# Moving number tables into an earlier stage, 16-bit one-hots, and a bias folded into a matmul as an extra row

## Chip, cores and metric

The kernel runs on one core of one Trainium2 chip. The metric is device time in microseconds (us), from one launch to its end; lower is better. Before the change it took 3679.51 us, the median of three runs.

## What is computed

Four layers follow one another on 3125 nodes with 256 features each; every layer works on the layernorm of x and adds its result to x.

```python
x = x + _L0_gnn_ref(_layernorm(x), edge_index, ...)   # two graph attention layers: 8 heads, then 1 head
x = x + _L0_ffn_ref(_layernorm(x)[None], ...)[0]      # 8 experts, top 2, 256 -> 512 -> 256, exact gelu
x = x + _L1_gnn_ref(_layernorm(x), src, dst, ...)     # attention over 100000 edges, then an MLP
x = x + _L1_ffn_ref(_layernorm(x)[None], ...)[0]      # shared MLP plus 4 experts, top 2
```

The part of the last layer that the change touches, and the routing of the second:

```python
# L1_ffn: E = 4 experts, 256 -> 128 -> 64 -> 256
o = jnp.einsum('ebag,ego->ebao', h, eW3) + eb3[:, None, None, :]
...
gates = softmax(x @ gW + gb); topv, topi = top_k(gates, 2); topw = softmax(topv)
gated = sum(sel * topw)          # out = shared + gated

# L0_ffn: E = 8 experts
top_vals, top_idx = jax.lax.top_k(logits, 2)
w = jax.nn.softmax(top_vals, axis=-1)
```

## The kernel before

The nodes are padded to 3200, that is 25 tiles of 128 (`NT`), or 5 chunks of 5 tiles (`NTC`, `TC`). x stays on chip (`X`), as does a transposed copy of the layer's input (`XT`). Each stage is a block with one instruction stream per engine, written out by hand; semaphores order them, and a stage ends with a barrier of all engines, after which POOL clears the stage's semaphores. The chain of a stage on VectorE (DVE) goes through `link`, which makes the next instruction wait for the one before.

The stages in order are: the edge lists are sorted and counted into a dense matrix of edge counts; graph layer with eight heads; graph layer with one head (`stage_gat_one_head`, L1053); first experts (`stage_experts`, L1395); attention (`stage_attention`, L1903); tail (`stage_tail`, L2211).

**One-head layer.** TensorE (PE) adds up weighted messages, chunk after chunk, 25 weight tiles each (L1319); DVE makes the weights (L1177) into a ring of six. At its start POOL makes a padding column (L1266, L1268) and then the greatest of all partitions (`partition_all_reduce`, L1271). After that POOL has nothing more to do in the stage. The router's logits, top values and indices of each chunk are made beside the next chunk.

**First experts.** The nodes are sorted by expert on the chip. POOL first makes number tables with `iota` (L1530 to L1537): numbers 0 to 127, three tables of node places, a table of spare rows; then a triangular table (`before`, L1540) from a table of ones that DVE sets (L1753). DVE waits for five of these before it reads the expert numbers (L1756); PE waits for all six before it ranks (L1567, L1569). DVE then works out each node's row, cuts it into a tile number and a place in the tile (L1787), and makes one-hots by comparing the number table with them:

```python
for j in range(2):
    hi    = (num[:, 0:TILES] == cutf[:, 1, half])     # L1790, 128x1425, bf16 out
    named = hi * parts[...]                            # L1793, twice, 128x1425
    lo    = (num[:, :] == cutf[:, 0, half])            # L1796, 128x3200
```

Here `num`, `cutf` and `parts` are 32-bit floats; the second operand is one number repeated over 57 or 128 elements. PE multiplies these one-hots (L1578), which gives the node of each row; DVE ends the list (L1808 to L1813), and POOL gathers the rows by indirect DMA (L1545). PE waits for all expert weights (`s_wt`) before the first tile's first layer (L1594). The weights, 8 MB, and two bias tables repeated over all partitions, 2 MB and 1 MB (L1500, L1501), are loaded by SP from the stage's start; then comes the diagonal of the counts (L1502), on which DVE waits at L1818. 57 tiles of rows pass through both layers, one after another.

**Tail.** For every chunk c the PE stream holds: the up matmuls of the MLP (L2357), the down matmuls (L2404), and, of chunk c-1, the last layer: `moe_up` (L2379) and `moe_down` (L2418) of the shared net "s" and of experts 0 to 3, interleaved. After the last chunk's MLP (c = 4) come chunk 3's experts, with the flips and router logits (L2336) of chunk 4 between them, and then chunk 4's experts. PSUM has a ring of three banks for up and three for down: PE can run three tiles ahead of the engine that reads. ScalarE (ACT) reads the up results (L2423, L2436); DVE reads the down results (L2498, L2556, L2559). DVE's order within a chunk c:

```python
norm(2, c - 1); finish_projection(c + 2); route(c - 1); norm(1, c + 2); add_features(c); finish_mlp(c)
add_expert_biases(c - 1)          # L2542: 20 instructions, L2546: the shared bias
if c == LAST_C: norm(2, LAST_C)
finish_moe(c - 1)                 # after the loop: route(LAST_C), add_expert_biases, finish_moe
```

`route` makes logits to weights of experts and needs two exponentials of ACT (L2445, L2449). ACT takes chunk 4's root (L2441) before chunk 3's expert reads, and chunk 4's exponentials among chunk 4's expert reads. The expert biases of the third layer (`tw.e3_b`) lie in all 128 partitions, loaded as a 512 KB broadcast during attention (L2173).

## Time and profile before

| | us |
|---|---|
| three runs | 3667.97, 3679.51, 3680.68 |
| median | 3679.51 |
| profiled execution, its own time | 3674.5 |
| its span, first to last instruction | 3672.7 |
| PE busy | 3043.4 (83% of the span) |
| DVE busy | 2850.6 (78%) |
| ACT busy | 2209.2 (60%) |
| POOL busy | 350.1 (10%) |

Of the span, the one-head layer takes 1481 to 1819, the first experts 1819 to 2186, attention 2186 to 3234 and the tail 3234 to 3673. All times of the trace count from the first instruction. A busy share says little by itself: each stage has its own limit, so the views below are of stretches. In a timeline a row stands for one instruction or a merged run of them, with its start, its duration, engine, line and tile names; the bracket tells how long the engine had been idle before it and whose end released it. PE's granted clock is given as a share of its full speed, 1.00 for 2.4 GHz and 0.50 for 1.2 GHz.

### The profile page before, as it was taken

The numbers are of one execution on the slowest core, as the hardware profiler recorded it, in microseconds if no ns is written. First come the engines' busy times: TensorE is split into PE (matmuls) and PEld (weight loads), VectorE is DVE, ScalarE is ACT, GpSimd is POOL, SyncE is SP. The second block draws the span as 40 slices with busy tenths as digits, with TensorE's granted clock in tenths as the row PEclk, the third lists the DMA queues.
The fourth block names the chain that finished last, engine by engine and source line by source line (L and its number), as shares of the span: only waits on it lengthen the run. The fifth ranks groups of instructions, "written<-read, shape, count | busy, mean of one in ns | idle before, by whom it ended". The sixth has DMA issues, their size and how long they took to land. (4 is left out here: it accounts for less than half of the span.)

```text
span 3672.7 us, 45213 instructions
## 1 busy us (share of the span) xinstructions
PE 3043.4 (83%) x15824; PEld 1562.9 (43%) x15826; DVE 2850.6 (78%) x3424; ACT 2209.2 (60%) x3171; POOL 350.1 (10%) x490
## 2 busy tenths in 40 slices
PE   3216766888888888899669969999999999969987
PEld 2212333333333333688547643333333333357765
DVE  8887987799999998455454459999999999934554
ACT  3101467899999998111123348889888888824332
POOL 0000000001111112000034400010111111000000
PEclk8557998999999999999879989999999999989998
DMA  2000234444443443444232154333333333210000
GB/s 55 0 0 23 78 145 156 125 117 117 113 117 108 117 113 90 177 144 151 76 114 65 57 194 112 88 88 89 90 89 88 89 89 89 69 62 22 8 8 14
DMA packets 191828, 325.64 MB, mean 89 GB/s; under 512 B 33388, under 2 KB 137046, under 8 KB 191632
## 3 DMA queue, kind: packets, MB, share of 16 engines
q1 hardware_dynamic: 175408, 294.36, 26.7%
q0 software_dynamic: 16224, 28.69, 2.8%
q8 instruction: 120, 1.97, 0.2%
q14 instruction: 76, 0.62, 0.1%
HBM read 254.53 MB, written 61.88 MB: 86 GB/s over the span
## 5 line engine op out<-in xcount | busy, mean ns | idle before, releaser
L921 PE MATMUL acc<-weights_then_messages,messages 128*64 128x400 f32 x3200 | 608.3, 513 | 93.7 <-DVE weights_then_messages L995 66.3
L2006 PE MATMUL acc<-weights,keys_and_values 128*64 128x400 f32 x3200 | 631.9, 516 | 2.4 <-DVE weights L2138 1.2
L2135 DVE SCALAR_TENSOR_TENSOR weights<-x,counts 128x1600 f32<-128x1600 f32 x304 | 555.0, 1826 | 18.0 <-ACT x L2102 7.6
L995 DVE SCALAR_TENSOR_TENSOR weights_then_messages<-rho,kappa,counts 128x800 f32<-128x800 f32 x400 | 415.0, 1082 | 4.8 <-PE acc L921 4.4
L2099 ACT ACTIVATE x<-scores 128x800 f32<-128x800 f32 x496 | 408.7, 851 | 13.5 <-PE scores L1993 13.4
L921 PEld LDWEIGHTS acc<-weights_then_messages,messages 128*64 128x64 f32 x3200 | 206.9, 137 | 491.7 <-issue 210.1
L1993 PE MATMUL scores<-q,keys_and_values 32*128 32x400 f32 x3200 | 386.5, 552 | 32.6 <-ACT x L2097 31.8
L943 ACT ACTIVATE weights_then_messages<-rho,wx 128x800 f32<-128x800 f32 x400 | 361.9, 953 | 26.0 <-DVE weights_then_messages L1000 17.2
L1000 DVE TENSOR_TENSOR weights_then_messages<-weights_then_messages,counts 128x1600 f32<-128x1600 f32 x200 | 365.0, 1825 | 5.4 <-ACT weights_then_messages L948 5.4
L2006 PEld LDWEIGHTS acc<-weights,keys_and_values 128*64 128x64 f32 x3200 | 195.1, 136 | 389.5 <-issue 347.9
L948 ACT ACTIVATE weights_then_messages<-weights_then_messages,kappa 128x800 f32<-128x800 f32 x400 | 360.5, 950 | 0.0
L2097 ACT ACTIVATE x<-scores,plus_minus_clip 128x800 f32<-128x800 f32 x304 | 283.4, 932 | 80.4 <-PE scores L1993 78.1
L651 PE MATMUL acc<-weights_then_messages 128*128 128x400 bf16 x1024 | 240.0, 370 | 102.4 <-ACT acc L627 59.1
L2102 ACT ACTIVATE x<-x,plus_minus_clip 128x800 f32<-128x800 f32 x304 | 296.9, 977 | 0.0
L1319 PE MATMUL acc<-weights_then_messages,weights 128*128 128x257 f32 x1250 | 278.7, 383 | 16.6 <-DVE weights L1177 12.7
L2126 DVE TENSOR_SCALAR x<-x 128x800 f32<-128x800 f32 (+1 forms) x400 | 267.4, 669 | 24.7 <-ACT x L2099 24.3
L1319 PEld LDWEIGHTS acc<-weights_then_messages,weights 128*128 128x128 f32 x1250 | 237.6, 191 | 52.4 <-DVE weights L1177 13.2
L1993 PEld LDWEIGHTS scores<-q,keys_and_values 32*128 32x128 f32 x3200 | 126.4, 185 | 288.5 <-ACT x L2097 213.7
L669 DVE TENSOR_TENSOR weights_then_messages<-dst_number_twofold,dst_of 128x6400 bf16<-128x6400 f16 x64 | 223.1, 3486 | 0.0
L625 ACT COPY counts_out<-acc 128x400 f32<-128x400 f32 x200 | 97.8, 489 | 197.4 <-PE acc L651 155.2
L651 PEld LDWEIGHTS acc<-weights_then_messages 128*128 128x128 bf16 x1024 | 119.5, 117 | 223.0 <-issue 183.8
L1177 DVE SCALAR_TENSOR_TENSOR weights<-rho,kappa,counts 128x640 f32<-128x640 f32 x125 | 109.4, 884 | 125.9 <-PE acc L1319 125.8
(371 smaller groups left out, 3642.6 us busy)
## 6 DMA issues: line engine op xcount, KB each, us to landing
counts<-edge_counts SPq DMA_DIRECT2D x200, 400.0 KB, 3.2
counts<-edge_counts SPq DMA_DIRECT2D x400, 200.0 KB, 2.4
edge_counts<-counts_out SPq DMA_DIRECT2D x40, 1000.0 KB, 4.1
counts<-edge_counts SPq DMA_DIRECT2D x24, 1600.0 KB, 7.1
w_first<-in_L_ffn_W_dram SPq DMA_DIRECT2D x8, 512.0 KB, 9.4
w_second<-in_L_ffn_W_dram SPq DMA_DIRECT2D x8, 512.0 KB, 8.8
y<-sums POOLq DMA_DIRECT2D x32, 100.0 KB, 2.7
denominators<-sums_of_weights POOLq DMA_DIRECT2D x32, 100.0 KB, 4.0
```

Source lines behind the costliest of these rows:

```text
L651: nc.tensor.matmul(acc[:, bass.ds(bank, 1), 0:CH], hot_s[:, u % 2, g, :, s], hot_d[:, u % 2, m // TWO, :, m % TWO], start=False, stop=Fals ...
L921: ins = nc.tensor.matmul(acc[64 * o:64 * o + 64, p, h, 0:CH], msg[:, t, r % 2 * Q + q, :], w[:, T % WR, q, half(h)], start=(t == 0), stop= ...
L943: nc.scalar.activation(mx[:, T % WR, e, :], rho[:, r % 2, 2 + e, :], ACT.Relu, bias=nkap[:, t, j:j + 1]).then_inc(s_relu, 1)
L948: nc.scalar.activation(mx[:, T % WR, e, :], mx[:, T % WR, e, :], ACT.Identity, bias=kap[:, t, j:j + 1]).then_inc(s_mx, 1)
L995: nc.vector.scalar_tensor_tensor(out=w[:, T % WR, q, :], in0=rho[:, r % 2, q, :], scalar=kap[:, t, j:j + 1], in1=cbuf[:, T % CR, :], op0=A ...
L1000: nc.vector.tensor_tensor(w[:, T % WR, 2:4, :], mx[:, T % WR, :, :], cbuf[:, T % CR:T % CR + 1, :].to_broadcast([P, 2, CW]), ALU.mult).the ...
L1319: ins = nc.tensor.matmul(acc[:, d, 0:F + 1], w[:, (i * NT + t) % WR, d * P:(d + 1) * P], msg[:, t, :], start=(t == 0), stop=(t == NT - 1))
L1993: ins = nc.tensor.matmul(sc[:, (n + j // 2) % SR, j % 2, 0:CH], kT[part, r % KF, t * P:(t + 1) * P], q[part, r % 2, :], start=True, stop=True)
L2006: ins = nc.tensor.matmul(acc[64 * e:64 * e + 64, p, 0:CH], msg[:, t, r % KF * 2 + p, D * e:D * e + 2 * D], w[:, U % WR, 2 * p + e, :], sta ...
L2099: nc.scalar.activation(out, pair, ACT.Exp, scale=D ** -0.5).then_inc(s_read, 1)
L2102: nc.scalar.activation(ex[:, U % XR, 0:2, :], ex[:, U % XR, 0:2, :], ACT.Exp, bias=ten[:, 1:2]).then_inc(s_ex, 1)
L2135: ins = nc.vector.scalar_tensor_tensor(out=w[:, U % WR, :, :], in0=out, scalar=EXP_HI, in1=counts, op0=ALU.min, op1=ALU.mult)
```

## The change

It does four things. (1) The number tables, the ones and the triangular table move from the experts' start into the one-head stage: POOL's five iotas and the triangular table stand behind `partition_all_reduce`, and DVE makes the ones and 16-bit copies of two tables at the end of chunk 1's weights. (2) The experts' waits for the tables go, and the one-hots read 16-bit tables and 16-bit row parts. (3) The third bias of the tail's experts becomes row 64 of the weight tile, against a row of ones under the hidden layer; the 20 DVE instructions per chunk go, and the shared bias is added earlier, behind `norm(2, c)`. (4) Chunk 4's routing moves: on DVE between chunk 3's experts 0 and 1, on ACT ahead of chunk 3's last up read.

```diff
@@ -1047,6 +1047,12 @@
...
+        self.num = core.sb(ctx, "numbers", [P, P])
+        self.num16 = core.sb(ctx, "numbers_16", [P, P], BF16)
+        self.parts16 = core.sb(ctx, "place_of_node", [P, 3, NT], BF16)
+        self.spare = core.sb(ctx, "spare_row", [P, TILES])
+        self.before = core.sb(ctx, "lower_ones", [P, P], BF16)
+        self.every = core.sb(ctx, "ones_16", [P, P], BF16)
...
@@ -1083,6 +1089,8 @@
...
+        parts = core.sb(ctx, "parts", [P, 3, NT])
+        s_const, s_const16 = core.sem("numbers_made"), core.sem("numbers_16_made")
...
@@ -1269,6 +1277,18 @@
...
+                nc.gpsimd.iota(route.num[:, :], pattern=[[1, P]], base=0, channel_multiplier=0,
+                               allow_small_or_imprecise_dtypes=True).then_inc(s_const, 1)
+                for j in range(2):
+                    nc.gpsimd.iota(parts[:, j, :], pattern=[[1, NT]], base=TILES + j * NT, channel_multiplier=0,
+                                   allow_small_or_imprecise_dtypes=True).then_inc(s_const, 1)
+                nc.gpsimd.iota(parts[:, 2, :], pattern=[[0, NT]], base=0, channel_multiplier=1,
+                               allow_small_or_imprecise_dtypes=True).then_inc(s_const, 1)
+                nc.gpsimd.iota(route.spare[:, :], pattern=[[P, TILES]], base=0, channel_multiplier=1,
+                               allow_small_or_imprecise_dtypes=True).then_inc(s_const, 1)
+                pool.wait_ge(s_const16, 1)
+                nc.gpsimd.affine_select(out=route.before[:, :], in_=route.every[:, :], compare_op=ALU.is_ge, fill=0.0, base=-1,
+                                        pattern=[[1, P]], channel_multiplier=-1).then_inc(s_const, 1)
...
@@ -1365,6 +1385,11 @@
...
+                        if i == 1 and t == NT - 1:
+                            dve.wait_ge(s_const, 5)
+                            nc.vector.memset(route.every[:, :], 1.0).then_inc(s_const16, 1)
+                            nc.vector.tensor_copy(route.num16[:, :], route.num[:, :]).then_inc(s_const16, 1)
+                            nc.vector.tensor_copy(route.parts16[:, :, :], parts[:, :, :]).then_inc(s_const16, 1)
...
@@ -1435,11 +1460,7 @@
...
-        before = core.sb(ctx, "lower_ones", [P, P], BF16)
-        every = core.sb(ctx, "ones_16", [P, P], BF16)
-        num = core.sb(ctx, "numbers", [P, P])
-        parts = core.sb(ctx, "place_of_node", [P, 3, NT])
-        spare = core.sb(ctx, "spare_row", [P, TILES])
+        before, every, num, num16, parts, spare = route.before, route.every, route.num, route.num16, route.parts16, route.spare
...
@@ -1450,7 +1471,7 @@
...
-        cutf = core.sb(ctx, "row_parts", [P, 2, S2])
+        cutf = core.sb(ctx, "row_parts", [P, 2, S2], BF16)
...
@@ -1462,9 +1483,9 @@
...
-        (s_wt, s_num, s_set, s_dve, s_pair, s_e, s_both, s_rank, s_tile, s_lo, s_named, s_ix, s_node,
+        (s_wt, s_dve, s_pair, s_e, s_both, s_rank, s_tile, s_lo, s_named, s_ix, s_node,
...
-             "weights_in", "numbers_made", "constants_set", "dve", "pair_ready",
+             "weights_in", "dve", "pair_ready",
...
@@ -1527,18 +1548,6 @@
...
-                nc.gpsimd.iota(num[:, :], pattern=[[1, P]], base=0, channel_multiplier=0,
-                               allow_small_or_imprecise_dtypes=True).then_inc(s_num, 1)
-                for j in range(2):
-                    nc.gpsimd.iota(parts[:, j, :], pattern=[[1, NT]], base=TILES + j * NT, channel_multiplier=0,
-                                   allow_small_or_imprecise_dtypes=True).then_inc(s_num, 1)
-                nc.gpsimd.iota(parts[:, 2, :], pattern=[[0, NT]], base=0, channel_multiplier=1,
-                               allow_small_or_imprecise_dtypes=True).then_inc(s_num, 1)
-                nc.gpsimd.iota(spare[:, :], pattern=[[P, TILES]], base=0, channel_multiplier=1,
-                               allow_small_or_imprecise_dtypes=True).then_inc(s_num, 1)
-                pool.wait_ge(s_set, 2)
-                nc.gpsimd.affine_select(out=before[:, :], in_=every[:, :], compare_op=ALU.is_ge, fill=0.0, base=-1,
-                                        pattern=[[1, P]], channel_multiplier=-1).then_inc(s_num, 1)
...
@@ -1562,7 +1571,6 @@
...
-                pe.wait_ge(s_num, 6)
...
@@ -1749,9 +1757,7 @@
...
-                nc.vector.memset(both[:, NT, :], 0.0)
-                nc.vector.memset(every[:, :], 1.0).then_inc(s_set, 2)
-                dve.wait_ge(s_num, 5)
+                link(nc.vector.memset(both[:, NT, :], 0.0))
...
@@ -1787,13 +1793,13 @@
...
-                    link(nc.vector.tensor_tensor(hi[:, half, :], num[:, 0:TILES].unsqueeze(1).to_broadcast([P, NT, TILES]),
+                    link(nc.vector.tensor_tensor(hi[:, half, :], num16[:, 0:TILES].unsqueeze(1).to_broadcast([P, NT, TILES]),
...
-                    nc.vector.tensor_tensor(lo[:, half, :], num[:, :].unsqueeze(1).to_broadcast([P, NT, P]),
+                    nc.vector.tensor_tensor(lo[:, half, :], num16[:, :].unsqueeze(1).to_broadcast([P, NT, P]),
...
@@ -2164,7 +2170,7 @@
...
-        self.e3, self.e3_b = core.sb(ctx, "w_expert_3", [P // 2, NE, F]), core.sb(ctx, "b_expert_3", [P, NE, F])
+        self.e3 = core.sb(ctx, "w_and_b_expert_3", [P // 2 + 1, NE, F])
...
@@ -2199,10 +2205,10 @@
...
-                bring(self.e3[:, e, :], a["L1_ffn_eW3"][e])
+                bring(self.e3[0:P // 2, e, :], a["L1_ffn_eW3"][e])
...
-            bring(self.e3_b[:, :, :], a["L1_ffn_eb3"].partition_broadcast(P))
+            bring(self.e3[P // 2:P // 2 + 1, :, :], a["L1_ffn_eb3"].unsqueeze(0))
...
@@ -2261,7 +2267,7 @@
...
-        eh2 = arena[0:P // 2, at_eh2:at_eh2 + NE * TN].rearrange("p (e n) -> p e n", n=TN)
+        eh2 = arena[0:P // 2 + 1, at_eh2:at_eh2 + NE * TN].rearrange("p (e n) -> p e n", n=TN)
...
@@ -2280,11 +2286,12 @@
...
-        (s_up, s_act, s_down, s_read, s_flip, s_turn, s_lg, s_logit, s_tb, s_feat, s_b2, s_eb, s_sb, s_dve, s_e1, s_e2, s_iota,
+        (s_up, s_act, s_down, s_read, s_flip, s_turn, s_lg, s_logit, s_tb, s_feat, s_b2, s_sb, s_dve, s_e1, s_e2, s_iota,
...
-             "bias_p_added", "features_added", "bias_2_added", "expert_biases_added", "shared_bias_added", "dve", "exp_1", "exp_2",
+             "bias_p_added", "features_added", "bias_2_added", "shared_bias_added", "dve", "exp_1", "exp_2",
...
+        s_row = core.sem("row_of_ones")
...
@@ -2430,7 +2437,7 @@
...
-                        to, b = (eh1[:, net, half(h)], tw.e1_b[:, net:net + 1]) if l == 1 else (eh2[:, net, half(h)],
+                        to, b = (eh1[:, net, half(h)], tw.e1_b[:, net:net + 1]) if l == 1 else (eh2[0:P // 2, net, half(h)],
...
@@ -2532,23 +2539,17 @@
             link(ins)
             link(nc.vector.tensor_tensor(wf[:, c % 2, :, :], hot[:, 0, :, :], hot[:, 1, :, :], ALU.add))
 
-        def add_expert_biases(dve, c):
-
-            for e in range(NE):
-                for j in range(TC):
-                    node = X[:, c * TC + j, :]
-                    if e:
-                        dve.wait_ge(s_eb, (c * NE + e - 1) * TC + j + 1)
-                    nc.vector.scalar_tensor_tensor(out=node, in0=tw.e3_b[:, e, :], scalar=wf[:, c % 2, j, e:e + 1], in1=node,
-                                                   op0=ALU.mult, op1=ALU.add).then_inc(s_eb, 1)
-            dve.wait_ge(s_eb, (c + 1) * NE * TC)
+        def add_shared_bias(dve, c):
+
+            dve.wait_ge(s_norm[1], (c + 1) * TC)
             nodes = X[:, chunk(c), :]
             nc.vector.tensor_tensor(nodes, nodes, tw.s3_b[:, :].unsqueeze(1).to_broadcast([P, TC, F]), ALU.add).then_inc(s_sb, 1)
 
-        def finish_moe(dve, c):
-
-            dve.wait_ge(s_sb, c + 1)
-            for net in ["s"] + list(range(NE)):
+        def finish_moe(dve, c, nets):
+
+            if "s" in nets:
+                dve.wait_ge(s_sb, c + 1)
+            for net in nets:
                 for j in range(TC):
                     n, node = down_no[(net, c, j)], X[:, c * TC + j, :]
                     dve.wait_ge(s_down, n + 1)
@@ -2587,6 +2588,7 @@
             @block.tensor
             def _(pe):
                 pe.wait_ge(tw.sem, tw.count)
+                pe.wait_ge(s_row, 1)
                 project(pe, 0)
                 project(pe, 1)
                 for g in range(3):
@@ -2660,18 +2662,18 @@
...
-                for n, (net, l) in enumerate(MOE_UPS):
+                            if n == len(MOE_UPS) - 2 and c == LAST_C:
+                                exp_gates(act, LAST_C)
+                                exp_pair(act, LAST_C)
+                for net, l in MOE_UPS:
...
-                    if n == 2:
-                        exp_gates(act, LAST_C)
-                    if n == 4:
-                        exp_pair(act, LAST_C)
...
+                nc.vector.memset(eh2[P // 2:P // 2 + 1, :, :], 1.0).then_inc(s_row, 1)
...
@@ -2679,6 +2681,7 @@
...
+                        add_shared_bias(dve, c - 1)
...
@@ -2687,15 +2690,15 @@
...
-                    if c:
-                        add_expert_biases(dve, c - 1)
...
-                    if c:
-                        finish_moe(dve, c - 1)
-                route(dve, link, LAST_C)
-                add_expert_biases(dve, LAST_C)
-                finish_moe(dve, LAST_C)
+                        add_shared_bias(dve, LAST_C)
+                        finish_moe(dve, LAST_C - 1, ["s", 0])
+                        route(dve, link, LAST_C)
+                        finish_moe(dve, LAST_C - 1, range(1, NE))
+                    elif c:
+                        finish_moe(dve, c - 1, ["s"] + list(range(NE)))
+                finish_moe(dve, LAST_C, ["s"] + list(range(NE)))
...
```

## Rows read from the trace of the kernel before

**Rows 1.** Page, parts 1 and 5 (busy, mean ns | idle before).
```profile
PE 3043.4 (83%) x15824; PEld 1562.9 (43%) x15826; DVE 2850.6 (78%) x3424; ACT 2209.2 (60%) x3171; POOL 350.1 (10%) x490
...
L1177 DVE SCALAR_TENSOR_TENSOR weights<-rho,kappa,counts 128x640 f32<-128x640 f32 x125 | 109.4, 884 | 125.9 <-PE acc L1319 125.8
```

**Rows 2.** Timeline, DVE, entry of the first experts.
```profile
1831.93 0.20 DVE L1756 CAST ids_f<-logits_values_ids 128x50 f32<-128x50 uint32 x1 [12.32 <-POOL spare_row L1537]
...
1860.10 0.21 DVE L1813 TENSOR_TENSOR place_of_row<-node_part,spare_row 128x57 uint32<-128x57 f32 x1
```

**Rows 3.** Timeline, POOL, and of DVE the instruction at 278.85.
```profile
1491.99 0.38 POOL L1271 PARTITION_ALL_REDUCE greatest<-top  x1 [10.20 <-issue]
...
1831.19 0.24 POOL L1530 IOTA numbers<- 128x128 f32 x1 [338.83 <-issue]
...
278.85 0.17 DVE L512 MEMSET ones<- 128x128 bf16 x1 [0.59 <-DVE keys L186]
...
286.05 0.98 POOL L485 IOTA step_number<- 128x1024 f32 x1 [179.51 <-issue]
...
317.13 0.46 POOL L592 IOTA column_number<- 128x400 f32 x1 [29.99 <-POOLq L482]
```

**Rows 4.** Timeline, PE and ACT, tail end, ahead of which PE idles.
```profile
3580.96 0.21 ACT L2441 ACTIVATE std<-std 128x5 f32<-128x5 f32 x1 [25.73 <-DVE std L2473]
...
3581.64 2.50 PE L2379 MATMUL up<-xt,w_shared 128*128 128x320 f32 x4 [9.57 <-ACT shared_hidden L2436]
...
3645.14 2.07 PE L2418 MATMUL down<-w_shared,shared_hidden 128*128 128x256 f32 x4 [10.96 <-DVE x L2556]
```

**Rows 5.** Timeline, entry of the experts; DMA issues (KB each, us to landing).
```profile
1838.55 2.95 SPq L1501 DMA_DIRECT2D keys_and_values<-in_L_ffn_b_dram  x1
...
1870.18 3.78 PE L1594 MATMUL up<-w_first,xt 128*128 x4
...
keys_and_values<-in_L_ffn_b_dram SPq DMA_DIRECT2D x1, 1024.0 KB, 14.0
```

**Rows 6.** Groups by form, DVE: count | busy us, mean ns | idle.
```profile
L669 DVE TENSOR_TENSOR weights_then_messages<-dst_number_twofold,dst_of 128x6400 bf16<-128x6400 f16 x64 | 223.1, 3486 | 0.0
L1796 DVE TENSOR_TENSOR xt<-numbers,row_parts 128x3200 bf16<-128x3200 f32 x2 | 7.0, 3486 | 0.0
L1793 DVE TENSOR_TENSOR xt<-keys_and_values,place_of_node 128x1425 bf16<-128x1425 bf16 x4 | 6.4, 1642 | 0.1
```

**Rows 7.** Timeline, DVE, biases of chunk 3 in chunk 4.
```profile
3569.21 8.00 DVE L2542 SCALAR_TENSOR_TENSOR x<-b_expert,expert_weights,x 128x256 f32<-128x256 f32 x20
3577.25 1.49 DVE L2546 TENSOR_TENSOR x<-x,b_shared 128x1280 f32<-128x1280 f32 x1
```

**Rows 8.** Windows: length, busy by engine, granted clock, DMA share, GB/s.
```profile
3582.00:3588.00 6.00, 6.00 (x13) 3.76 (x13) 1.13 (x4) 1.47 (x4) 0.00 (x0) 0.53 0.00 0
...
3645.00:3650.00 5.00, 4.86 (x12) 3.43 (x12) 1.59 (x5) 0.53 (x1) 0.00 (x0) 0.59 0.00 0
...
1880.00:2110.00 230.00, 228.13 (x998) 160.03 (x995) 100.69 (x168) 78.17 (x163) 104.16 (x107) 1.00 0.20 62
```

**Rows 9.** Timeline, PE, tail's start; group of a DVE memset.
```profile
3234.32 5.39 PE L2393 MATMUL down<-w_p,xt 128*128 128x256 f32 x12 [20.46 <-PEq L2056]
...
3241.35 4.58 PE L2393 MATMUL down<-w_p,xt 128*128 128x256 f32 x20 [1.65 <-DVE keys_and_values L2460]
...
L656 DVE MEMSET zero<- 128x400 f32 x1 | 0.4, 392 | 0.6 <-PEq L482 0.6
```

**Rows 10.** Timeline, ACT and DVE, routing of chunk 4.
```profile
3629.89 1.28 ACT L2445 ACT_TABLE_LOAD   x1
...
3631.31 1.93 ACT L2436 ACTIVATE keys_and_values<-up,b_expert 128x320 f32<-128x320 f32 x4
...
3631.44 0.17 DVE L2510 TENSOR_REDUCE per_node<-logits 128x5 f32<-128x20 f32 x1 [9.91 <-ACT logits L2445]
...
3634.88 0.18 DVE L2533 TENSOR_TENSOR expert_weights<-hot 128x20 f32<-128x20 f32 x1
```

## The prediction

> **What bounds the kernel now.** The page first: PE is busy for 83% of the span [rows 1]. Where PE is fed, taking work off another engine gives nothing; only the stretches count in which PE stands still. The change touches three: the entry of the first experts, the end of the tail and the tail's start.
>
> At the experts' entry the timeline of DVE shows one long chain. DVE stands still for 12.32 us ahead of its first cast, until POOL's spare-row table is there, and the node list ends at 1860.3 [rows 2]. POOL's timeline tells why: its first iota starts at 1831.19, and takes 0.24 us. The same kind of hole stands ahead of the iota at 286.05, in a stage that DVE had entered by 278.85, and 10.20 us stand ahead of the all-reduce at 1491.99, which comes behind other POOL operations. The iota at 317.13, with no all-reduce since the one before it, waited for the barrier alone [rows 3]. So I read that each switch between the all-reduce and the other operations costs POOL 7 to 12 us. At 1819 everybody waits for it.
>
> At the tail's end PE stands still twice: 9.57 us ahead of 3581.64, since ACT is held up in chunk 4's root (it waited 25.73 us for DVE, which was at the bias instructions), and 10.96 us ahead of 3645.14, since DVE was late with the routing and then the biases [rows 4]. In the chunks before, the bias instructions lie under PE's work.
>
> **Part 1, the tables.** POOL's tables take about 1 us, behind a switch that now falls at some 1492 to 1504, where POOL has nothing else to do. DVE adds three instructions of 0.2 us at the end of chunk 1 (about 1615), long after the tables it waits for; behind them are queued only the next weights. In this stage DVE waits longer for PE (125.9 us) than it works on weights (109.4) [rows 1], and the ring holds six, so they are covered; uncovered they would cost 0.6. POOL's iotas could hold up DVE at the layer's ramp by their own 1 us at most. I take 0, range 0 to 1.6. In the experts DVE then casts right at the start: 12.3 us earlier. PE's ranking and ACT's exponential stand behind DVE in this chain and move with it.
>
> What is late next? PE's first expert matmul at 1870.18 comes 9.9 us behind the end of the list: gather, flip, turn. With the list ready at 1848.0 it would come at 1857.9. It also waits for the weights: the last bias table was issued at 1838.55 and landed 14.0 us later, at 1852.6 [rows 5]. So the weights are no bound, by 5 us; but the first gather starts 4.6 us before they are in, and shares the DMA engines with them. That costs 0 to 4.6 us; most of the gather's time lies behind, so I take 1. SP's and POOL's later transfers of the stage keep their order. **Gain at the entry: 12.3 - 1 = 11.3 us.**
>
> **Part 2, 16-bit one-hots.** The chain has two compares of 3486 ns and six operations on 1425 elements (the four products at 1642 ns, two compares of that size taken alike): 16.8 us, nearly all on the path. They take one element per step: 3486 ns for 3200. The one row with 16-bit operands throughout does 6400 in the same time, but its number tables are kept twofold, so that both operands lie in neighbouring elements [rows 6]. Here the second operand stays one number repeated. The bounds are 0 and, with the per-element part halved, some 7.8 us. The instructions themselves are the nearest rows, as they have the repeated operand, and the fast row's extra tables would be pointless if a repeated operand were as good. I take 0. The 16-bit row parts (L1787) cost as before.
>
> The Trainium skill, "Vector Engine (DVE) Microarchitecture Reference", section 5.1, speaks against this part: it asks for a step of one in every operand and reports that one element read 16 times, in a two-source operation on 2-byte data, ran at the slow rate. By that the term is 0 too; no row here shows this case.
>
> **Part 3, the bias as a row.** The 512 KB less to load lie in attention, where SP loads ahead of use: 0. The 65th row adds no column to a matmul: 0. The shared bias, 1.49 us, stands earlier, where DVE next waits for PE's projections; covered by PE's up matmuls, 1.49 us a chunk if they were not. In chunks 1 to 3 the 8.0 us of biases were under PE's work: 0.
>
> Chunk 4 counts. The root's input comes 8.00 + 1.49 us earlier [rows 7], so ACT is free at about 3571.8, just when PE has filled its three banks (3581.64 - 9.57 = 3572.1). Of the idle 0.3 remain: **gain 9.3**. The idle also cost clock: in the 6 us after it PE was busy throughout at a mean grant of 0.53, so 2.8 us of work were lost, 3.0 with the piece before [rows 8]. **Gain 3.0.**
>
> At the tail's start there is a loss. PE now waits for the row of ones: DVE sets 2560 elements, in one partition. 400 took 392 ns, so about 2.5 us; PE starts up to 2.7 us later than at 3234.32. But it waited 1.65 us for DVE at 3241.35 anyway [rows 9]. Bounds 0 and 2.7; I take the difference of 1.1, and 0.4 since the clock rises later: **loss 1.5**.
>
> **Part 4, the router.** In the last chunk DVE has neither routing nor biases left, so PE's 10.96 us go: **gain 11.0**. Behind that idle the grant was 0.59 over 4.86 busy us: **gain 2.0** [rows 8]. But the routing now stands in chunk 4, ahead of expert 1's down reads. PE cannot pass three unread tiles. From the up matmul of expert 2's second layer on come ACT's read (about 0.5, 1.93 for four), a table load of 1.28, the exponential 0.2, the routing from L2510 to the end of L2533, 3.6, and the first tile's read, 0.4: 6.0 us [rows 10]. PE fills three tiles meanwhile, about 1.5 us (two took 2.07 at the low level [rows 4]). **New stall 4.5**; queued behind it are expert 1's last two tiles and the rest of PE's stream, and behind ACT's exponentials its last up read. Whether so short an idle costs clock no row tells: bounds 0 and 3.0, and I take a **loss of 2.0**, the smaller of the two drops seen.
>
> Tail: 9.3 + 3.0 + 11.0 + 2.0 - 4.5 - 2.0 - 1.5 = 17.3 us. Both: 28.6 us. From the profiled execution's own 3674.5 (its span of 3672.7 and 1.8 around it) that gives **3645.9 us**. The median of the three runs stands 5.0 us above that execution; seen from it, the same gain gives 3650.9, which the range must hold.
>
> **Rivals.** *A, the one-hots do run at double rate* (10%). The list is ready 7.8 us earlier still, but PE waits for the weights until 1852.6 [rows 5], and the gathers start in the thick of the loads. At most 5.3 us more than 1857.9; with the same gather delay, 4: 3642. The fast 16-bit row speaks for it, its layout against it.
>
> *B, the tail gives most of it back* (14%). DVE reaches the routing late, the stall is twice as long (9.0), costs the full 3.0 of clock and 3 us more for a second drop, the start costs 2.7: 9.3 + 3.0 + 13.0 - 9.0 - 6.0 - 2.7 = 7.6. With 11.3 that is 18.9: 3655.6; with 4.6 lost in the gathers, 3659.2. For it speaks that PE, DVE and ACT now wait for each other in turn; against it that the routing's input is ready while PE still has two up matmul groups ahead.
>
> *C, slower* (4%): the clock in the expert loop. PE is busy there for 228 of 230 us at a mean grant of 1.00 [rows 8], some 4.1 us for each of 57 tiles. At half level a tile would take up to 4 us more. If the level, after an entry under the loads, did not hold, the gain would be used up from 8 tiles on, and from 12 tiles it would be slower by 0.5%. 20 tiles give 3646 + 80 = 3726. Against it: the loop held the level throughout, and the change leaves it as it is.
>
> *D, the hole is no switch* (3%) but something that POOL does when it first works in this stage, also now, ahead of the gather. From 1848 on it would cost up to 12 us again: 3657. Against it the iota at 317.13.
>
> **How the numbers follow.** The forecast's own case has 69%. With no gather delay, no clock lost behind the new stall and a free start of the tail it gives 3641.4; with 4.6, 3.0, 2.7 and 1.6 for the one-head layer 3653.3. The median may stand 5.0 us above such a sum, as it does now, and the three runs spread over 12.7: so 3637 to 3658. For 8 in 10 I take 3636 to 3660; that holds A, nearly all of the own case and part of B. A measurement of this kernel can tell about 0.5%, 18.4 us of the median, from no change, so the border is at 3661. Faster: own case, A, and those parts of B and D that stay below it, 0.83; within: the rest of these, 0.13; slower: C, 0.04.
>
> **What would show it.** Right: DVE's first cast within 1 us of the stage's start; the first L1594 some 11 us closer to that start; L1790, L1793 and L1796 at 1642 and 3486 ns; L2542 gone; under 1 us of idle among chunk 3's shared up matmuls; one stall of about 5 us at L2418 in chunk 4 and none in the last chunk. Wrong: a hole ahead of the first gather, one-hots in half their time, a stall above 8 us, or half-level clock in the expert loop.

## The result, and the profile after

The changed kernel takes 3639.2 us (median of 4 runs, 3637.5 to 3645.2) beside 3678.9 for the kernel before on the same chip; the ratio is 0.9903, 95% interval 0.9886 to 0.9921. In a later set of five rounds it was 3641.6 beside 3679.4, ratio 0.9895 (0.9880 to 0.9910). The forecast was 3645.9, range 3636 to 3660. The profiled execution of the changed kernel took 3645.2 us (span 3643.4), the slowest of its four; the profiled one before took 3674.5. So the two traces are 29.3 us apart where the sum said 28.6; the table shows that so close a match is luck.

A first table says where this went. A stage begins with SP's first DMA issue in it; the last column runs from TensorE's first up product of chunk 3's mixture (its shared net and four experts), which stands in chunk 4, to the end of the span. All in us, one profiled execution each; "after, again" is a second run of the changed kernel, and the rows below it are the other experiments.

| kernel | one-head | experts | attention | tail | its last part |
|---|---|---|---|---|---|
| before | 338.2 | 366.4 | 1048.6 | 438.4 | 104.0 |
| after | 337.4 | 353.8 | 1049.9 | 416.6 | 82.4 |
| after, again | 337.4 | 353.6 | 1048.3 | 418.0 | 82.4 |
| b_dummy_iota | 336.5 | 351.4 | 1048.5 | 441.8 | 104.3 |
| a_twofold | 338.1 | 354.7 | 1046.6 | 416.6 | 82.3 |
| a_route_late | 336.6 | 356.6 | 1048.2 | 409.4 | 76.3 |
| a_route_late_early_exp | 336.6 | 353.6 | 1048.1 | 410.2 | 74.6 |
| a_exps_earlier | 338.3 | 354.8 | 1046.6 | 409.2 | 75.1 |
| a_64rows | 338.4 | 354.5 | 1046.5 | 428.6 | 91.5 |
| a_late_row_wait | 337.1 | 353.7 | 1046.5 | 424.7 | 89.6 |
| a_warm_front | 337.0 | 353.9 | 1046.7 | 416.3 | 82.3 |
| a_warm_reduce | 329.8 | 354.5 | 1050.2 | 416.4 | 82.4 |
| a_all_four | 328.3 | 352.5 | 1048.3 | 411.5 | 76.3 |

Between before and after: experts 12.7 us shorter, tail 21.9 shorter, attention 1.3 longer (it spreads over 4 us in kernels that do not touch it), one-head 0.8 shorter, and 4.7 us more in the stages ahead, which the change leaves alone (in the kernels that leave them alone the one-head stage starts anywhere from 1475.3 to 1485.8). So the three stages that the change touches got 35.3 us shorter, 6.7 more than the sum, and 6.0 us of drift elsewhere hid it. On the page TensorE's work has not moved, and VectorE lost 36 us of work (compare [rows 1]).

Page of the changed kernel, parts 1 and 5 (busy, mean ns | idle before).
```profile
PE 3040.4 (83%) x15825; PEld 1560.8 (43%) x15826; DVE 2815.1 (77%) x3327; ACT 2209.9 (61%) x3171; POOL 347.1 (10%) x490
...
L1185 DVE SCALAR_TENSOR_TENSOR weights<-rho,kappa,counts 128x640 f32<-128x640 f32 x125 | 109.3, 883 | 124.4 <-PE acc L1339 124.4
```
The weights of the one-head layer cost what they did: the tables added there are covered.

The experts' entry, timelines of POOL (one-head stage), then VectorE and TensorE (experts' stage, which starts at 1823.18).
```profile
1496.96 0.38 POOL L1279 PARTITION_ALL_REDUCE greatest<-top  x1 [10.46 <-issue]
1508.34 0.24 POOL L1280 IOTA numbers<- 128x128 f32 x1 [11.01 <-issue]
...
1823.38 0.20 DVE L1762 CAST ids_f<-logits_values_ids 128x50 f32<-128x50 uint32 x1
...
1831.20 1.65 DVE L1796 TENSOR_TENSOR keys_and_values<-numbers,row_parts 128x1425 bf16<-128x1425 bf16 x1
1836.00 3.48 DVE L1802 TENSOR_TENSOR xt<-numbers,row_parts 128x3200 bf16<-128x3200 bf16 x1
...
1860.26 3.46 PE L1602 MATMUL up<-w_first,xt 128*128 x4
```
The hole of 11.01 us now stands behind the all-reduce, where nobody waits. The first cast comes 0.2 us into the stage (12.65 before, [rows 2]), the one-hots take what they took [rows 6], and the first expert matmul comes 37.1 us into the stage instead of 50.9 [rows 5]: 13.8 us earlier. The last first-layer matmul comes 14.1 us earlier; 1.4 of that go back at the stage's end, which leaves 12.7. 0.6 of the 1.4 lie in the first key projections, which take 4.4 us instead of 3.8; why was not tried.

The tail's end, timelines of ACT, PE and DVE.
```profile
3563.86 0.21 ACT L2448 ACTIVATE std<-std 128x5 f32<-128x5 f32 x1 [16.30 <-DVE std L2480]
...
3589.38 1.28 ACT L2452 ACT_TABLE_LOAD   x1
3590.68 0.22 ACT L2452 ACTIVATE logits<-logits 128x20 f32<-128x20 f32 x1
...
3590.93 0.18 DVE L2517 TENSOR_REDUCE per_node<-logits 128x5 f32<-128x20 f32 x1 [4.96 <-ACT logits L2452]
...
3595.13 2.08 PE L2425 MATMUL down<-w_and_b_expert,keys_and_values 65*128 65x256 f32 x4 [4.83 <-DVE x L2560]
...
3616.58 2.42 PE L2425 MATMUL down<-w_shared,shared_hidden 128*128 128x256 f32 x10
```
Both idle times of [rows 4] are gone; one of 4.83 us is new, in chunk 4. Behind it the granted clock is low. Windows of PE: length, busy, granted clock, DMA share, GB/s.
```profile
3593.00:3595.00 2.00, 0.00 (x0) 0.71 0.00 0
3595.00:3597.00 2.00, 1.87 (x4) 0.50 0.00 0
3597.00:3599.00 2.00, 2.00 (x5) 0.50 0.00 0
3599.00:3601.00 2.00, 2.00 (x5) 0.59 0.00 0
3601.00:3603.00 2.00, 2.00 (x11) 1.00 0.00 0
```
PE was busy 5.87 us in the last three low windows at 0.50, 0.50 and 0.59: 2.8 us of work lost. The tail's start, DVE and PE, the stage starting at 3226.85:
```profile
3227.83 2.19 DVE L2676 MEMSET keys_and_values<- 1x2560 f32 x1 [7.61 <-POOL iota L2567]
...
3230.17 9.74 PE L2400 MATMUL down<-w_p,xt 128*128 128x256 f32 x32 [23.95 <-DVE keys_and_values L2676]
```
PE starts 3.3 us into the tail instead of 0.04 [rows 9], but its first up product of chunk 0 comes only 0.9 later (25.03 for 24.11). In the other kernels with this tail start it comes at 24.8 to 25.1, in one, a_route_late, at 23.9.

### The profile page after: what moved, and what is told of

Its sections match the earlier page's. It is cut to its first block and busy times, and to the rows that moved or that the text cites. A ratio compares the mean times of both kernels' runs of the same rounds, so it can differ in the third digit from the quotient of the medians.

```text
span 3643.4 us, 45117 instructions
## 1 busy us (share of the span) xinstructions
PE 3040.4 (83%) x15825; PEld 1560.8 (43%) x15826; DVE 2815.1 (77%) x3327; ACT 2209.9 (61%) x3171; POOL 347.1 (10%) x490
## 5 line engine op out<-in xcount | busy, mean ns | idle before, releaser
L1185 DVE SCALAR_TENSOR_TENSOR weights<-rho,kappa,counts 128x640 f32<-128x640 f32 x125 | 109.3, 883 | 124.4 <-PE acc L1339 124.4
```

## The experiments

Theory S: POOL pays 10 to 12 us for a switch between the all-reduce and its other operations, and part 1 gained because the switch now falls where POOL is idle. Theory R: a repeated 16-bit operand keeps VectorE at one element a step. Theory N: part 4 loses time once parts 1 to 3 are in. The rivals stand with each run. Four, four and three kernels shared a chip; times are ratios to the kernel before on that chip.

**b_dummy_iota.** On the kernel before:
```
 nc.gpsimd.partition_all_reduce(most[:, :], top_es[:, :], P, RMAX).then_inc(s_all, 1)
+nc.gpsimd.iota(small[:, :], pattern=[[0, 1]], ...)      # one column, read by nobody
```


> The kernel before with one thing added: a one-column iota on POOL right behind the one-head stage's all-reduce; every table stays in the experts' stage. Theory S (a switch): POOL pays some 10 to 12 us whenever its next work is an iota, memset or select and the one before was the all-reduce, and pays it ahead of that work wherever it stands. Then the one-column iota starts 10 to 11.5 us behind the all-reduce, POOL's first iota in the experts' stage starts within 1.5 us of the stage's first DMA issue where it was 12, the first cast is 10.5 to 11.5 us earlier in the stage, the experts' stage takes 354 to 356 us instead of 366.4, and the whole is 10 to 12.5 us shorter (about 3667). Rival D of the prediction (the hole belongs to POOL's first work of a stage, whatever was before): the first iota still stands 12 us into the stage and the whole is within 2 us of the kernel before.

3659.5 us, ratio 0.9954 (0.9938 to 0.9971), so 17 us faster, 11 to 23. POOL's timeline, both stages:
```profile
1493.02 0.38 POOL L1273 PARTITION_ALL_REDUCE greatest<-top  x1 [10.01 <-issue]
1504.26 0.14 POOL L1274 IOTA small<- 128x1 f32 x1 [10.87 <-issue]
...
1819.15 0.24 POOL L1534 IOTA numbers<- 128x128 f32 x1 [314.76 <-POOLq L1265]
```
One iota that computes nothing of use moves the hole: the tables' iota starts 0.3 us into the experts' stage (11.9 before) and the first expert matmul comes at 36.6 us, even a little ahead of the changed kernel's 37.1. Rival D is out. All that parts 1 and 2 gain at the entry is this switch, and one line gets it. The size was above the expectation: the gather came 11.7 us earlier, the matmul 14.3. From the gather's issue to the first flip it is 5.4 us instead of 7.5: gathers issued while the weights were still landing were not slower here. The total is 17 us by the medians, but 12.1 from trace to trace, and the tail, which the edit leaves alone, is 3.4 longer in this trace.

**a_twofold.** On the changed kernel, shortened (the same for the compares of 58 and for `named`, whose places are doubled too):
```
-cutf = core.sb(ctx, "row_parts", [P, 2, S2], BF16)
+cutf = core.sb(ctx, "row_parts", [P, 2, S2, 2], BF16)      # each value twice, side by side
-num16[:, :].unsqueeze(1).to_broadcast([P, NT, P]), cutf[:, 0, half].unsqueeze(2).to_broadcast([P, NT, P])
+counted(P), twice(cutf[:, 0, half, :], P)      # both seen as [P, NT, P // 2, 2]
```


> The changed kernel with the one-hots' repeated operand laid out in pairs: every row part and every place stands twice side by side, so that the innermost step of both operands is one 16-bit element and the repeat moves one dimension out; 57 columns become 58. Theory R (the prediction's ground for part 2: a 16-bit operand that is repeated with step 0 keeps the engine at one element a cycle, a pair layout does not): the 3200-element one-hot takes 1.75 to 1.9 us instead of 3.49 and the 1450-element ones 0.8 to 1.0 instead of 1.64, the first gather is issued 7 to 8.5 us earlier in the stage. Rival F (16-bit operands give this operation nothing in any layout): 3.49 and 1.67 stay. In the time even theory R gives little, 0 to 2 us, since VectorE's wait for the diagonal ends at 38 us of the stage whatever comes before it, and the first hidden layer's bias stands behind it.

3642.4, ratio 0.9912 (0.9887 to 0.9937): the same as the changed kernel. Timelines, DVE and PE:
```profile
1831.05 1.82 DVE L1814 TENSOR_TENSOR xt<-numbers,row_parts 128x3200 bf16<-128x3200 bf16 x1
1832.79 0.91 DVE L1809 TENSOR_TENSOR keys_and_values<-numbers,row_parts 128x1450 bf16<-128x1450 bf16 x1
...
1841.06 0.21 DVE L1831 TENSOR_TENSOR place_of_row<-node_part,spare_row 128x57 uint32<-128x57 f32 x1
...
1858.47 3.44 PE L1604 MATMUL up<-w_first,xt 128*128 x4 [8.79 <-DMA keys_and_values<-in_L_ffn_b_dram]
```
Theory R holds: 1.82 us for 3.48, 0.91 for 1.65. The Trainium skill, "Vector Engine (DVE) Microarchitecture Reference", section 5.1, asks for an innermost step of one in every operand, and reports the slow rate for one element read 16 times in a two-source operation on 2-byte data. The pair layout meets the first, the changed kernel's is the second, and the rows agree with both. But the list, 7.4 us earlier, buys nothing: PE waits 8.79 us for the last bias table, and starts 38.3 us into the stage. So the weights and biases are the entry's next bound, and the changed kernel stands close to it: the table landed at 35.7 us of its stage, 1.4 ahead of the first product, and in three of the runs (a_twofold, a_route_late, a_exps_earlier) it landed at 37.5 to 37.8 and PE's first product waited for it, until 38.0 to 38.3.

**a_route_late and a_route_late_early_exp.** On the changed kernel:
```
 VectorE (shortened):
-finish_moe(dve, LAST_C - 1, ["s", 0]); route(dve, link, LAST_C); finish_moe(dve, LAST_C - 1, range(1, NE))
+finish_moe(dve, LAST_C - 1, ["s"] + list(range(NE))); route(dve, link, LAST_C)
 ScalarE, last read loop; the two calls ahead of chunk 3's last up read go:
+if n == 2: exp_gates(act, LAST_C)      # early_exp: n == 0
+if n == 4: exp_pair(act, LAST_C)       # early_exp: n == 1
```


> The changed kernel with its fourth part undone: the last chunk's routing stands behind the whole of chunk 3's mixture again, with its two exponentials behind the last read loop's third and fifth entries, as in the kernel before; the shared bias's place, the row of ones and the tables stay. Theory N (part 4 is a net loss): with the row of ones the routing ends soon enough. Chunk 3's mixture has no stall (4.83 us gone, and the dip of the clock after it, some 2.9), the last chunk has one of 1 to 2.5 us at its shared down matmuls and a dip of 0 to 2 after it; the tail takes 411 to 414 us instead of 416.6 and the whole is 3 to 6 us faster than the changed kernel (3633 to 3636). Rival W (part 4 is worth what it was made for): the 10.96 us stall of the kernel before comes back with its 2 us of clock and the whole is 4 to 6 us slower than the changed kernel.

> As a_route_late, with the two exponentials behind the first and second entries of the last read loop. Theory N: VectorE has the gates' scores ready about 1 us after the last expert of chunk 3 is added, ScalarE answers about 4 us later and the routing ends some 9 us after its start, ahead of the shared down matmuls, which come 12 us after it. No stall of over 1 us is left in the last 50 us, the granted clock stays at 1.00 there, the tail takes 408 to 410 us and the whole is 6 to 8.5 us faster than the changed kernel (3631 to 3633). Rival W: no faster than the changed kernel, since the stall only moves.

a_route_late: 3630.2, ratio 0.9882 (0.9857 to 0.9906). a_route_late_early_exp: 3632.5, ratio 0.9877 (0.9850 to 0.9905). One fence for each; PE of the first, DVE of the second:
```profile
3597.62 1.56 PE L2425 MATMUL down<-w_shared,shared_hidden 128*128 128x256 f32 x6
3600.58 1.13 PE L2425 MATMUL down<-w_shared,shared_hidden 128*128 128x256 f32 x4 [1.39 <-DVE x L2557]
```
```profile
3597.75 0.17 DVE L2517 TENSOR_REDUCE per_node<-logits 128x5 f32<-128x20 f32 x1 [5.40 <-ACT logits L2452]
...
3604.07 2.07 DVE L2557 TENSOR_TENSOR x<-x,down 128x256 f32<-128x256 f32 x5 [2.70 <-PE down L2425]
```
With the routing back where it was, the stall is 1.39 us and costs no clock; with ScalarE's exponentials two and three places earlier it is none, and VectorE waits for PE. The last part falls from 82.4 to 76.3 and 74.6. The tail of a_route_late is shorter than was expected (409.4 against 411 to 414). Theory N holds: part 4 costs some 6 to 8 us against leaving the routing alone. What had made the 10.96 us of [rows 4] were the 8 us of biases, which part 3 takes away without it. (The intervals of the three ratios overlap; the traces carry this, and the medians say the same.)

**a_exps_earlier.** On the changed kernel, the routing left in chunk 4:
```
-if n == len(MOE_UPS) - 2 and c == LAST_C: exp_gates(act, LAST_C); exp_pair(act, LAST_C)
+if n == len(MOE_UPS) - 4 and c == LAST_C: exp_gates(act, LAST_C)
+if n == len(MOE_UPS) - 3 and c == LAST_C: exp_pair(act, LAST_C)
```


> The changed kernel with the routing left in chunk 4 and only ScalarE's order changed: the first exponential two reads earlier (behind expert 1's second layer, where ScalarE waits 5.15 us for TensorE), the second one read earlier. If the 4.83 us stall is VectorE's wait of 4.96 us for that exponential and nothing of the routing itself, the first exponential ends 3.2 us earlier, VectorE's wait for it falls to about 1.7, the stall to 1 to 2 us and the clock's dip behind it to 0 to 2: the whole 4 to 7 us faster than the changed kernel. Rival: the reads that the table load delays hold TensorE up as long; then within 1.5 us of it.

3632.2, ratio 0.9873 (0.9858 to 0.9888), where the changed kernel has 0.9895 on the same chip. Timelines, ACT, DVE, PE:
```profile
3574.24 1.28 ACT L2452 ACT_TABLE_LOAD   x1
3578.82 0.22 ACT L2452 ACTIVATE logits<-logits 128x20 f32<-128x20 f32 x1 [3.30 <-DVE logits L2515]
...
3579.07 0.17 DVE L2517 TENSOR_REDUCE per_node<-logits 128x5 f32<-128x20 f32 x1 [0.29 <-ACT logits L2452]
...
3583.28 1.13 PE L2425 MATMUL down<-w_and_b_expert,keys_and_values 65*128 65x256 f32 x4 [0.16 <-DVE x L2560]
```
The stall is 0.16 us and the whole 9.4 us faster than the changed kernel, both better than expected (1 to 2, 4 to 7). It is less since the table load too went into ScalarE's idle time: it does not wait for the exponential's input. So the loss of part 4 is not the routing's place but the place of two exponentials in ScalarE's order. A routing ahead of expert 1's reads is covered if ScalarE answers at once.

**a_64rows.** On the changed kernel:
```
-x, w = eh2[:, net, j * P:(j + 1) * P], tw.e3[:, net, :]
+x, w = eh2[0:P // 2, net, j * P:(j + 1) * P], tw.e3[0:P // 2, net, :]
```


> The changed kernel with its experts' down products over the first 64 rows of weights and hidden values, as before the change: the row of ones and the bias row stay in place but are not used, so the experts' third bias is left out of the output. Theory T (a product over 64 rows costs TensorE something at each change between it and the 128-row products around it; 65 rows do not): the up group behind a down group goes back from 2.32 to about 2.42 us for 8 products and from 3.37 to 3.57 for 12, and the tail is 0.5 to 2.5 us longer than the changed kernel's 416.6. Rival V (the small regain per chunk in the tail came from VectorE's 400 bias additions that are gone): the groups stay as in the changed kernel and the tail within 0.4 us of it. The whole within 3 us of the changed kernel by either.

This kernel leaves the experts' third bias out of the output; it is here for TensorE's time alone. 3651.2, ratio 0.9936 (0.9911 to 0.9962). PE timelines of chunk 1's mixture in the changed kernel, then in this one:
```profile
3435.22 2.43 PE L2425 MATMUL down<-w_and_b_expert,keys_and_values 65*128 65x256 f32 x10
3437.48 2.32 PE L2386 MATMUL up<-xt,w_expert 128*128 128x320 f32 x8
3439.73 1.29 PE L2386 MATMUL up<-keys_and_values,w_expert 128*64 128x320 f32 x4
```
```profile
3432.92 2.42 PE L2425 MATMUL down<-w_and_b_expert,keys_and_values 64*128 64x256 f32 x10
3435.27 2.42 PE L2386 MATMUL up<-xt,w_expert 128*128 128x320 f32 x8
3437.62 1.29 PE L2386 MATMUL up<-keys_and_values,w_expert 128*64 128x320 f32 x4
```
From start to start the down group takes 2.26 us with 65 rows and 2.35 with 64, the up group behind it 2.25 and 2.35; the second down group, with a 64-column up group behind it, takes 2.35 in both. A whole chunk's mixture is 31.59 us with 65 rows and 31.86 with 64, here as in the kernel before: 0.27 a chunk, and theory T stands against V. The total misses the bound of 3 us: the last part is 9.1 us longer than the changed kernel's. Nearly all of it is the clock: there the granted clock was at half level for 6.8 us behind the 20 products of four columns and for 17.1 behind the 4.83 us stall, in the changed kernel for none and 6.8; half of the 17.1 us more is 8.5.

**a_late_row_wait.** On the changed kernel:
```
 pe.wait_ge(tw.sem, tw.count)
-pe.wait_ge(s_row, 1)
 ...
 moe_down(pe, c - 1, "s")
+if c == 1: pe.wait_ge(s_row, 1)
```


> The changed kernel with one wait moved: TensorE waits for the row of ones ahead of the first expert's down products in chunk 1 instead of at the tail's start. If the memset of the row (2.2 us at the tail's start) is what delays the tail by 0.9 us, TensorE starts its first projection within 0.2 us of the stage's start instead of 3.3, the first up product of chunk 0 stands 24.1 us into the tail instead of 25.0, and the tail is 0.5 to 1.2 us shorter. Rival: VectorE, which makes the row before its own first work, sets it; then TensorE starts sooner but the first up product stays at 25.0.

The first projection starts 0.04 us into the tail and the first up product at 24.28 instead of 25.03, as expected (a_all_four, with the same edit, has 24.3). Yet the kernel takes 3646.7 us (3645.7 to 3648.3 in all four runs), ratio 0.9923 (0.9897 to 0.9948), and its last part is 7.2 us longer than the changed kernel's. PE around the same 4.83 us stall:
```profile
3576.46 2.29 PE L2343 MATMUL flip<-w_gate,xt 128*128 128x4 f32 x20
3578.62 3.57 PE L2386 MATMUL up<-xt,w_expert 128*128 128x320 f32 x8
...
3590.20 2.08 PE L2425 MATMUL down<-w_and_b_expert,keys_and_values 65*128 65x256 f32 x4 [4.83 <-DVE x L2560]
...
3594.53 8.90 PE L2425 MATMUL down<-w_and_b_expert,keys_and_values 65*128 65x256 f32 x20
```
And its clock:
```profile
3577.00:3581.00 4.00, 4.00 (x23) 0.84 0.00 0
3581.00:3585.00 4.00, 4.00 (x13) 0.74 0.00 0
3585.00:3589.00 4.00, 0.37 (x2) 1.00 0.01 2
...
3593.00:3597.00 4.00, 4.00 (x10) 0.50 0.00 0
...
3601.00:3605.00 4.00, 4.00 (x10) 0.50 0.02 7
```
The clock drops to the lower of its levels (1.2 GHz) right behind the 20 products of four columns each, and again behind the stall, there for some 17 us instead of 7 (the low windows, each by its share of the way to 0.50). The stall is the same to 0.01 us. So what a stall costs in clock is not in its length alone: the kernel whose tail starts 0.75 us earlier, and that was expected to gain 0.5 to 1.2, lost 7. The clock accounts for it (half of 13.7 us more at half level is 6.9); that the earlier start is the cause is not shown. a_64rows shows the same pattern; after, after again, a_twofold, a_warm_front and a_warm_reduce have the short one. Why it falls one way or the other was not tried.

**a_warm_front and a_warm_reduce.** On the changed kernel, the first:
```
 nc.gpsimd.partition_all_reduce(allm[:, :], top[:, :], P, RMAX).then_inc(s_all, 1)      # stage_front
+nc.gpsimd.iota(small[:, :], pattern=[[0, 1]], ...)
```
the second, shortened, at the end of POOL's work in stage_gat_aggregate (the pad's memset and select leave the one-head stage):
```
+nc.gpsimd.memset(route.small ...); nc.gpsimd.memset(route.pad ...); nc.gpsimd.affine_select(out=route.pad ...)
+nc.gpsimd.partition_all_reduce(route.small[:, 1:2], route.small[:, 0:1], P, RMAX)      # read by nobody
```


> The changed kernel with a one-column iota added right behind the first all-reduce, some 180 us before the stage of steps begins with an iota of 1024 columns. Theory S (a switch of POOL between the all-reduce and iota, memset or select, paid ahead of the next work of the other kind): the step numbers' iota starts 1 to 2 us after the last merge instead of 8.5, VectorE's wait of 8.8 us for it shrinks to under 2, and the whole is 7 to 8.5 us faster than the changed kernel. Rival D (the hole comes with a stage's first POOL work): the 8.8 us wait stays and the whole is within 2 us.

> The changed kernel with the pad of the one-head stage made at the end of POOL's work of the stage before, where POOL waits 14 us, and behind it an all-reduce of one column that nobody reads. Theory S, in the other direction: the hole of 10.46 us ahead of the one-head stage's all-reduce goes into that idle time; the all-reduce starts 0.5 to 1.5 us after VectorE's reduction, TensorE's idle time of 12.96 us ahead of its first aggregation shrinks to 3 to 4, and the whole is 8.5 to 10.5 us faster than the changed kernel. Rival: what clears the semaphores between two stages on POOL, or the stage's start, undoes the warming; then the hole stays and the whole is within 2 us.

a_warm_front: 3632.1, ratio 0.9883 (0.9857 to 0.9909). VectorE's wait for the step numbers, in the changed kernel and then in this one, and POOL's small iota, behind an all-reduce that ended at 106.7:
```profile
288.88 0.69 DVE L515 CAST step_number<-step_number 128x1024 f16<-128x1024 f32 x1 [8.80 <-POOL tile_number L487]
...
113.77 0.13 POOL L234 IOTA small<- 128x1 int32 x1 [7.09 <-issue]
...
280.23 0.69 DVE L518 CAST step_number<-step_number 128x1024 f16<-128x1024 f32 x1 [1.18 <-POOL tile_number L490]
```
The wait of 8.80 us is 1.18: 7.6 us gained, as theory S says and against D; the switch itself took 7.09 us here. The wait is the evidence: the ratio's interval overlaps the changed kernel's. a_warm_reduce: 3636.4, ratio 0.9894 (0.9869 to 0.9920). POOL:
```profile
1473.01 0.38 POOL L985 PARTITION_ALL_REDUCE small<-small  x1 [6.06 <-issue]
1483.60 0.35 POOL L1283 PARTITION_ALL_REDUCE greatest<-top  x1 [10.21 <-DVE top L1266]
1495.28 0.24 POOL L1284 IOTA numbers<- 128x128 f32 x1 [11.33 <-issue]
```
The switch, 6.06 us here (behind a select), is paid in POOL's idle time, the real all-reduce starts 0.1 us behind VectorE's reduction, and the stage is 7.6 us shorter, 1 less than the bound expected: PE's clock was at half level until 1495, and its row products took 4.60 us instead of 2.39. The whole does not show it (8.5 to 10.5 us were expected): the ratio is the changed kernel's own. The stages around it are at the long end of their spread in the profiled execution; whether the dummy work plays a part in that was not tried. Both directions of the switch are now seen, and a semaphore clear or a stage's start between two all-reduces does not undo it.

**after_again and a_all_four.** The changed kernel itself; and a_route_late_early_exp, a_late_row_wait, a_warm_front and a_warm_reduce together.

> The changed kernel itself, beside the two below on the same chip. Expected 3637 to 3645. In its last 50 us the 4.83 us stall comes again; the stretch at the lower clock behind it is 7 us long if it is fixed by the program, and anything from 7 to 15 if it depends on when the stall falls, as the runs so far suggest (7 us in three kernels whose routing stands in chunk 4, 15 in two others with the same 4.8 us stall).

> The changed kernel with four edits at once: the last routing behind chunk 3's mixture with its exponentials behind the first and second reads, the wait for the row of ones at the first expert's down products, the small iota behind the first all-reduce, and the pad with its idle all-reduce in the stage before the one-head stage. If the four parts lie in stretches that do not overlap, their sizes add: tail 416.6 less 7.5 less 0.75, 409 or shorter; step numbers 7.6 earlier; one-head stage 329.8 instead of 337.4. Together 23 us less than the changed kernel, 3614 to 3619. Rival: TensorE's clock gives half of it back, being low when it starts earlier; then 3624 to 3630.

3641.6 and 3620.9 us (3611.1 to 3627.5), ratios 0.9895 (0.9880 to 0.9910) and 0.9843 (0.9824 to 0.9863): the four edits are 20.7 us faster than the changed kernel and 58 than the one before. Expected were 3614 to 3619. By the traces it is 7.0 before the one-head stage, 9.1 in it, 1.1 in the experts and 6.6 in the tail, 23.7, where 23 were expected: the parts add within what these stages differ by from one execution to the next, and the median gives 3 less. In after_again the low clock behind the stall is short again. In a_all_four, which has no stall, the 20 narrow products still drop the clock:
```profile
3563.71 2.29 PE L2350 MATMUL flip<-w_gate,xt 128*128 128x4 f32 x20
3565.86 3.63 PE L2393 MATMUL up<-xt,w_expert 128*128 128x320 f32 x8
```

## Why the prediction was right, point by point

- **The switch** (entry, 11.3 forecast, 13.8 measured at the first expert matmul, 12.7 left with the stage's end). Right in mechanism and shown by three kernels. The gather is issued 12.5 us earlier (12.3 forecast). The gather's delay of 1 us is the step that was wrong: it took 0.8 us less under the loads, and another 0.5 fell away between first flip and first product.
- **"The weights are no bound, by 5 us"** was too sure. It took the landing at 33.3 us of the stage from the trace of before. In the changed kernel it landed at 35.7, 1.4 us ahead of the product at 37.1, and in other runs at up to 37.8. It cost nothing here only because the list was no earlier. Why it moved is open. The gathers alone do not explain it: in b_dummy_iota, with the first gather at the same 29 us, it landed at 33.7, and in the 9 us before the first gather (from 19 to 28) the queues moved 400 GB/s in the kernel before and 401 in b_dummy_iota, but 372 in the changed one.
- **Part 2 at nothing**: right. The row's rate is unchanged, and a_twofold shows the repeated operand to be the reason. Rival A priced a faster list at 4 us; it gives nothing.
- **Part 1 in the one-head layer at nothing**: right (124.4 us of waiting for PE left).
- **Part 3**: the root's idle time is gone (0.1 us left) and with it the clock's drop, 9.3 + 3.0 as forecast. The row of ones cost 0.9, forecast 1.5. The line "the 65th row adds no column to a matmul: 0" missed a gain of 0.27 us a chunk.
- **Part 4**, the step that was wrong: 11.0 and 2.0 gained; the new stall 4.83, forecast 4.5; its clock 2.8, forecast 2.0, near the upper bound of 3.0. The gain was credited to part 4. The runs split them otherwise: without part 4 only 1.39 of the 10.96 us come back. The sum was right, its attribution was not: nearly all of the 13 us belongs to part 3, and part 4 is a loss of some 6 to 8. That the number came out all the same is luck: the change has both parts, so it did not matter which one was credited.
- No step had the drop of the clock which the kernel before shows behind its 20 narrow products (0.59 and 0.56 from 3604 to 3612, 3.4 us of work) and the changed one does not; a_late_row_wait, a_64rows and a_all_four show that it can come back, so whether the change or chance took it away is open. With it the tail adds up: 9.5 + 3.0 + 11.0 + 2.0 - 4.8 - 2.8 - 0.9 + 5 x 0.27 + 3.4 = 21.8, and 21.9 were measured. The forecast 17.3 was short mainly by this drop and the 65 rows.
- Rivals B, C and D: the stall was not twice as long, the expert loop ran at a grant of 1.00, and no hole stands ahead of the first gather.
- **The total** came out 6.7 us below the forecast because its sum starts from a profiled execution below the median before and ends at one above the median after; trace against trace it is 0.7 off, by luck, as the table shows. By the medians the change is worth 39.7 us, by the interval 29 to 42; the runs of one kernel spread over 2 to 22, and how much of that is TensorE's clock was not tried.

## What to carry to other kernels

When POOL idles 6 to 12 us ahead of a trivial instruction, ask what kind of work it did last; if one of the two is an all-reduce and the other is not, put one dummy instruction of the new kind where POOL is idle, and leave the real work where it is. When a change has a part that removes a late engine's work and one that moves the rest of it out of the way, build the first alone before keeping the second. And when routing must go through another engine, place that engine's answer in its order first; its table load can be hidden ahead of the wait.

## What the runs showed of the hardware

- POOL between all-reduce and iota, memset or select: 10.0 to 11.3 us in the one-head stage in either direction, 7.1 behind the first all-reduce of the kernel, 6.1 and 6.7 where it ran at the end of the stage before the one-head stage; none between two all-reduces across a stage's end.
- VectorE, a compare of 3200 16-bit elements: 0.57 ns per element with the repeated operand stored as pairs, 1.09 with one element repeated.
- TensorE: a group of ten 64-row down products and the 128-row up group behind it each take 0.1 us more than with 65 rows; the whole mixture of a chunk takes 0.27 more.
- TensorE's granted clock after the same 4.83 us of idle was low for 7 us in five executions of four kernels and for some 17 in two others, and the 20 products of four columns were followed by the lower level in some executions and not in others, though the engine was busy throughout.
- A memset of 2560 elements in one partition took 2.19 us, 0.86 ns each.
